# Row sums of the global attention spread over their 32 partitions by a VectorE shuffle in place of a TensorE matmul

## What is computed

```python
q = _split_heads(inputs @ Wq + bq, B, S)
k = _split_heads(inputs @ Wk + bk, B, S)
v = _split_heads(inputs @ Wv + bv, B, S)
scores = jnp.einsum('bhqd,bhkd->bhqk', q, k) * scale
weights = jax.nn.softmax(scores, axis=-1)
attn = jnp.einsum('bhqk,bhkd->bhqd', weights, v)
attn = attn.transpose(0, 2, 1, 3).reshape(B, S, D)
return attn @ Wo + bo
```

## Time and profile before

| | us |
|---|---|
| median of 3 runs | 8890.2 |
| lowest and highest run | 8887.18, 8890.36 |
| the profiled execution | 8895.99 |
| its span, first to last instruction | 8893.9 |

### The profile page before, as it was taken

One profiled execution on the slowest core, in us unless ns is written; L12 is line 12 of the kernel. 1 busy time (PEld: TensorE's weight loads), 2 busy tenths in 40 slices (PEclk: granted clock), 3 DMA queues, 4 the chain that ended last, 5 costly groups with the idle time before them and its releaser, 6 DMA issues.

```text
span 8893.9 us, 389467 instructions
## 1 busy us (share of the span) xinstructions
PE 8528.5 (96%) x173512; PEld 4534.7 (51%) x173512; DVE 7401.2 (83%) x12442; ACT 6567.1 (74%) x13653; POOL 3024.4 (34%) x3001
## 2 busy tenths in 40 slices
PE   5789999999999999999999999999999999999998
PEld 4445554555545555455554555545555455544543
DVE  5578888888888888888888888888888888889985
ACT  2367777777777777777777777777777777777877
POOL 5514442244412444034440444304443144420000
PEclk8899999999999999999999999999999999999999
DMA  1120101201011010110102001120101200111000
GB/s 46 35 56 20 26 22 28 48 19 29 26 38 31 21 28 25 44 29 19 26 26 56 18 22 28 28 47 17 26 26 28 48 16 24 27 27 32 9 10 8
DMA packets 312022, 253.97 MB, mean 29 GB/s; under 512 B 97244, under 2 KB 303052, under 8 KB 308300
## 3 DMA queue, kind: packets, MB, share of 16 engines
q1 hardware_dynamic: 310348, 229.05, 10.7%
HBM read 136.82 MB, written 78.05 MB: 24 GB/s over the span
## 4 chain that ended last, share of the span: by engine, by line
PE 86%; DVE 6%; ACT 3%; issue 3%; POOL 2%; DMA 0%; SPq 0%; POOLq 0%; ACTq 0%; DVEq 0%
PE PS L1239 23%; PE PS L1172 23%; PE PS L1224 20%; PE PS L967 7%; PE PS L1024 5%; PE PS L1031 4%; DVE block_max L1700 3%; PE PS L1038 2%; PE PS L1016 1%; ACT PB L1455 1%; ACT tail L1373 1%; DVE NM L1578 1%; PE PS L999 1%; PE PS L1081 0%; DVE X L1630 0%
## 5 line engine op out<-in xcount | busy, mean ns | idle before, releaser
L1700 DVE TENSOR_REDUCE block_max<-PS 128x1 f32<-128x512 f32 (+1 forms) x9632 | 6126.6, 682 | 932.4 <-PE PS L1172 859.8
L1455 ACT ACTIVATE PB<-PS 128x448 f32<-128x448 f32 (+1 forms) x11200 | 5385.4, 544 | 1556.8 <-PE PS L1224 1535.9
L1224 PE MATMUL PS<-QP,KP 99*32 99x448 bf16 x43904 | 4307.2, 354 | 64.9 <-ACT PB L1455 43.5
L1172 PE MATMUL PS<-KP,QP 96*32 96x512 bf16 (+1 forms) x43904 | 3998.8, 355 | 26.4 <-issue 18.6
L1239 PE MATMUL PS<-PB,VA 128*32 128x448 f32 x22400 | 2689.0, 539 | 5.3 <-issue 4.5
L1224 PEld LDWEIGHTS PS<-QP,KP 99*32 99x32 bf16 x43904 | 1417.8, 97 | 1247.4 <-issue 471.8
L1172 PEld LDWEIGHTS PS<-KP,QP 96*32 96x32 bf16 x43904 | 1291.3, 96 | 1400.1 <-issue 532.6
L880 POOL TENSOR_TENSOR SC<-SC,NM 128x1120 f32<-128x1120 f32 x210 | 433.1, 2062 | 1633.4 <-DVE NM L1578 1633.3
L1239 PEld LDWEIGHTS PS<-PB,VA 128*32 128x32 f32 x22400 | 791.0, 110 | 377.3 <-issue 4.4
L852 POOL TENSOR_TENSOR QB<-Qn,C 128x896 f32<-128x896 f32 x392 | 666.9, 1722 | 11.8 <-ACT Qn L1310 11.8
L902 POOL CAST shift_parts<-shift 14x128 bf16<-14x128 f32 x112 | 31.5, 281 | 1747.6 <-ACT shift L1366 1747.6
(11 more groups left out here) (116 smaller groups left out, 4801.9 us busy)
## 6 DMA issues: line engine op xcount, KB each, us to landing
QP<-q_dram SPq DMA_DIRECT2D x672, 56.0 KB, 2.1
VP<-vT_padded SPq DMA_DIRECT2D x448, 70.0 KB
k_dram<-k_parts SPq DMA_DIRECT2D x56, 336.0 KB, 3.0
KP<-k_dram SPq DMA_DIRECT2D x336, 56.0 KB, 2.1
q_dram<-q_parts SPq DMA_DIRECT2D x56, 336.0 KB, 2.8
KP<-k_dram SPq DMA_DIRECT2D x48, 392.0 KB, 6.1
VA<-v_dram SPq DMA_DIRECT2D x16, 816.0 KB, 4.6
vT_padded<-SC SPq DMA_DIRECT2D x112, 112.0 KB
```

Source lines behind the costliest of these rows:

```text
L1172: ins = mm(PS[at:at + QT, bank, n * width:(n + 1) * width], QP[0:ROWS, Q_SLOTS[k % AUNITS], t:t + QT], KP[0:ROWS, g, t // BLK, keys], star ...
L1224: ins = mm(PS[k0:k0 + 32, bank, 0:BLK], KP[0:ROWSM, k // NBLK, h, c * P + k0:c * P + k0 + 32], QP[0:ROWSM, Q_SLOTS[k], h * BLK:(h + 1) * B ...
L1455: S.activation(exp_buffer(k, c)[0:n, h, :], PS[0:n, at % ST_BANKS, 0:BLK], ACT.Exp, scale=float(ADIM) ** -0.5).then_inc(exp_done, 1)
L1700: V.tensor_reduce(block_max[:, k % 2, queries.start:queries.stop, j], tile, AX.X, ALU.max).then_inc(max_read, 1)
```

## The change

The spread of the row sums becomes a DVE instruction, `stream_shuffle`: in each group of 32 partitions every output partition takes input partition 16 (`ADIM`). It reads `tail[:, 0]` and writes `tail[:, 1]` in SBUF, without PSUM. It stands in chunk 1's first half-place on DVE, behind the chunk's first maxima tile, and waits for `attn_read`, for the last user of `tail[:, 1]` (`normed3`, a wait that ACT had before) and for POOL's product of the unit before (`attn_normed`). The Ln of `invert` reads `tail[:, 1]` in place of the bank, and stays where it was on ACT. `spread` no longer uses `SIDE_BANK`, so the task after it waits for the reader of the task before it.

```diff
 SIDE_READER = {...
-               "q2": "act", "v2": "dve", "spread": "act", "project": "dve", "mean3": "dve", "var3": "act",
+               "q2": "act", "v2": "dve", "project": "dve", "mean3": "dve", "var3": "act",
...
-            self.fix(t + 1, 1, "spread", k)
+            self.fix(t + 1, 0, "spread", k)
             self.fix(t + 1, 1, "invert", k)
...
-            if task == "spread":
-                return sums_log, of(b, 0, AUNITS, i)
...
-                def spread(k, bank):
-
-                    pe.wait_ge(attn_read, of(b, 0, AUNITS, k))
-                    across(bank, pick_sum, tail[:, 0, :]).then_inc(sums_spread, 1)
-
...
                 def invert(k):
 
                     act.wait_ge(sums_spread, of(b, 0, AUNITS, k))
-                    wait(act, normed3, thirds_before(b, k))
-                    S.activation(tail[:, 1, :], PS[:, SIDE_BANK, 0:BLK], ACT.Ln).then_inc(sums_log, 1)
+                    S.activation(tail[:, 1, :], tail[:, 1, :], ACT.Ln).then_inc(sums_log, 1)
...
+                def spread(k):
+                    dve.wait_ge(attn_read, of(b, 0, AUNITS, k))
+                    wait(dve, normed3, thirds_before(b, k))
+                    wait(dve, attn_normed, of(b, 0, AUNITS, k - 1))
+                    V.stream_shuffle(tail[:, 1, :], tail[:, 0, :], [ADIM] * 32).then_inc(sums_spread, 1)
```

More of the change, by code:

```diff
@@ L1143, in do @@
                         v2(i, bank)
-                    elif task == "spread":
-                        spread(i, bank)
                     elif task == "project":
@@ L1674, in do @@
                         v2(i, bank)
+                    elif task == "spread":
+                        spread(i)
                     elif task == "project":
```

## The result

The changed kernel takes 8784.66 us (median of four runs, 8783.44 to 8788.9) against 8890.28 us of the kernel before (four runs beside it, 8887.18 to 8893.08). The ratio is 0.9882, with a 95% interval of 0.9865 to 0.9899: 105.6 us less. The forecast was 8814, its range 8790 to 8850. The sign was right, and the gain was larger than the range allowed.

A forecast was written before the change was run, and what follows sets the result against it. PE was taken as the bound, busy 96% and holding 86% of the chain. 84 + 10 - 14 - 4 = 76 us less than the profiled execution gave 8820, so 8814 for the median; range 8790 to 8850.

The forecast's parts named there:

- PE's time: At 112 ends of units, the spread's matmuls leave PE, 0.75 us each: 84.0 us less.
- hidden anyway: Rival: PE had slack at the spread's place, so removing it leaves the time at 8890; chance 0.06.
- The shared bank: PE's weight loads no longer wait for the Ln to free the bank at ends of units: 10 us less.
- What ACT gives back: Behind the Ln, ACT comes 0.69 us earlier, PE asks for 0.84; over 94 exponential waits, 14 us return.
- What DVE gives back: The shuffle queues ahead of maxima tiles that PE waits for; DVE's idle time falls short, 4 us return.
- the 0.87 that the place allowed: At one end of a unit, a shuffle of up to 0.87 us delays no maxima that PE needs.
- The plan's moves: Moved tasks, once in each of seven images, cost nothing; 8 us at most if their cover fails.
- ACT gives nothing back: Rival: the 94 exponential waits lie elsewhere or have enough lead, full 94 us gain, 8796; chance 0.13.
- DVE becomes the bound: Rival: the shuffle takes 1.31 us, as long as NM, delaying maxima at ends of units; about 8852, chance 0.17.
- slower: Rival: a slow shuffle, say 2.0 us, delays the maxima's banks by 127 us against 94 gained; 8923, chance 0.04.

The follow-up runs named there:

- e1: The kernel before, with the spread's four matmuls made twice in a row: 8966.01 us, ratio 1.0078.
- e3: The changed kernel with the old spread's half-place kept empty and PE's next task again waiting for the Ln: 8788.29 us, ratio 0.9883.
- e4: The changed kernel without the shuffle, ACT squaring the unspread sums in place of the Ln: 8789.37 us, ratio 0.9884.
- e2: The changed kernel with the old spread's half-place kept empty in the plan, so no other task moves into it: 8789.32 us, ratio 0.9882.
- e5: The changed kernel with the shuffle made twice, one after the other: 8821.27 us, ratio 0.9921.
- e6: The changed kernel with the Ln also waiting for chunk 1's last scores, at all ends of units but the very last: 8808.72 us, ratio 0.9908.

## Why the prediction missed, point by point

Two steps of the sum failed. It had no term for where PE's instructions lie, which made 16 to 22 of the 105.6 us, and it let ACT give back 14 us where the runs show about 1. The terms in turn:

**PE's time (84 us) was right.** e1 adds 83.5 us in chunk 1 for 84.0 of work, and in after chunk 1 is 74.9 us shorter and chunk 2 another 12.8. The rule that the prediction weighed as a rival ("hidden anyway", from the Trainium skill, Perfetto Trace Analysis, "Identifying the Most-Contended Engine") fell with it: weight loads at 51% didn't mean that half of PE was free, since work added at this place costs its full duration. The chain at the place decided.

**The shared bank (10 us) was right in kind and near in size: some 7 us.** In before the Ln did stand in the chain. In e3 the wait is still there with 39.1 us on the weight loads, and of these 7.6 us are lost in chunks 0 to 2, beside an early Ln. The prediction's excess over the plain wait, 10 of 41.4 us, thus came near; what the wait cost beside the late Ln of before was not measured by itself. Together with PE's slot that would be 91 us, and the counts above give 83 to 90.

**What ACT gives back (14 us) was the term most mis-sized: it is about 1.** The prediction took 0.72 us of idle time away from the Ln, added 0.03 for the longer instruction, and let ACT come 0.69 us earlier against PE's 0.84. The timeline of the last image, before (with the exponentials ahead of it):

```profile
8269.83 2.28 ACT L1455 ACTIVATE PB<-PS 128x448 f32<-128x448 f32 x5
...
8273.86 1.83 ACT L1455 ACTIVATE PB<-PS 128x448 f32<-128x448 f32 x4
```

and after:

```profile
8170.70 2.28 ACT L1445 ACTIVATE PB<-PS 128x448 f32<-128x448 f32 x5
...
8171.67 0.67 DVE L1618 STREAM_SHUFFLE tail<-tail 128x448 f32<-128x448 f32 x1
...
8172.82 0.62 ACT L1363 ACTIVATE tail<-tail 128x448 f32<-128x448 f32 x1
...
8173.47 0.58 ACT L1365 ACTIVATE tail<-tail 128x448 f32<-128x448 f32 x1
...
8173.95 1.83 ACT L1445 ACTIVATE PB<-PS 128x448 f32<-128x448 f32 x4
```

From the one exponential to the other, ACT needs 8273.86 - 8269.83 = 4.03 us before and 8173.95 - 8170.70 = 3.25 after: 0.78 earlier, not 0.69. All 112 ends agree: the mean from the last exponential ahead of the Ln to the next work behind its reciprocal is 2.40 us before and 1.62 after, 0.78 less. The reason is at 8172.82: without a wait the Ln starts 0.16 us before the exponentials ahead of it end (8170.70 + 2.28 = 8172.98). An idle gap that closes gives back more than its own length, since the overlap comes with it. Of PE's 0.84 that leaves 0.06 us, and by 94 waits 6 us at the most; the waits grew by 0.9 us. The shuffle is done at 8172.34, 0.48 us ahead of the Ln, so the added wait between DVE and ACT was met with room, as predicted.

**What DVE gives back (4 us) was nothing.** The shuffle took 0.68 us with its mask for the forecast's 0.62, under the 0.87 that the place allowed, and DVE's mean in the windows, 8.91, stayed under the prediction's 7.64 + 1.46 = 9.10. The allowance of 4 us was a choice without a row, and e4 shows that it should have been 0. The estimate from the Trainium skill (VectorE: DVE Perf Modes, "The perf-mode tier table"), 0.73, was as near as the trace's from the other side, and made no difference.

**The plan's moves cost little:** some 3 us at most (e2), under the 8 that the prediction allowed.

**The step that isn't in the sum at all is PE's instructions.** The prediction subtracted its terms from runs of before, whose trace held 26.1 us of stalls that belonged to the placement, and put at nothing what the edit does to the place of PE's instructions. With every term at its measured size, 83 to 90 us together, the forecast would have been 8800 to 8807: the terms account for some 7 to 14 us more than the 76 forecast, chiefly ACT's 14 and DVE's 4 that weren't given back, and the time would still lie inside the range. The other 16 to 22 us, where the borders fell, took it out. The chain had shown "issue" at 3%, and the prediction gave it no bound. An edit of PE's program of this size moves this kernel by up to some 30 us (8779 to 8809 in after), as much as the whole band of 8800 to 8830 that the forecast had for itself.

Of the rivals, "ACT gives nothing back" (8796, at 0.13) is what happened on the engines: PE's waits for exponentials hardly grew. That the mean over the placements is 8795.4 is luck in part, since before's placements held 6.7 us more of stalls than after's. "DVE becomes the bound" needs a shuffle about twice as long (e5), and "slower" one still longer.

## What to carry to other kernels

Work on the engine that the chain runs through at the place costs and gives back its whole duration there; the waits of its weight loads (here 7 of 39 us were lost), the share of another engine in the chain and a small overload of that engine need an experiment, or a row, before they get a number in the sum. An experiment's total can hide a few us behind an accident of placement, as e3's did; compare the stretch where the edit works. Closing an engine's idle gap gives back the gap and the overlap of neighbours. Before a difference of 0.3% in a long unrolled program is put down to an edit, shift the program's start by a few dozen instructions in both kernels and compare the means.

## What the runs showed of the hardware that was not expected

- PE can stand still for up to 3.62 us between two matmuls of one group, and starts again soon after a block of instructions has landed. Moving PE's whole program by 63 to 191 instructions moved the time by up to 30 us (8779.42 to 8809.35). The Trainium skill (Runtime: NRT & Kernel Launch, "Instruction fetch mechanics") describes blocks of 16 KiB and takes their fetch to be hidden behind the pace at which instructions are issued. The size agrees with the trace (22.28 MB in 1360 packets); the hiding holds for most blocks here, but 30 of before's 1367 were followed by a stall of PE.
- The shuffle of 128 x 448 f32 takes 647 to 684 ns, 667 in the mean, for a fixed source in each group of 32 partitions, and issues an instruction for its mask of 14 ns.
- ACT's Ln on SBUF shows 601 ns on average in after, where it follows an exponential without a gap, and 578 in e6, where it mostly has waited; and yet the former is the faster course: it starts before the one ahead has ended (8172.82 against 8172.98).
